# One tile a round fetched by SyncE row by row, the lows spread by ScalarE, and nodes laid out by 56 to a partition, in a graph layer on one NeuronCore

## The reference

```python
msg = relu(x[src] + edge_attr @ We + be)            # 200000 x 128
aggr = segment_sum(msg, dst, num_segments=6250)
h = (1.0 + eps) * x + aggr
h = relu(h @ W1 + b1) @ W2 + b2
h = (h - mean(h, 0)) * rsqrt(var(h, 0) + 1e-5) * gamma + beta
out = layernorm(x + (relu(h) + x))
```

## Time and profile before

| | |
|---|---|
| median of 3 runs | 1557.24 us (1556.69 to 1558.63) |
| the profiled execution | 1564.18 us, its span 1562.2 us |
| PE busy | 1416.0 us (91%), 23435 matmuls |
| ACT busy | 1255.7 us (80%) |
| POOL busy | 1160.5 us (74%), 1179 gathers |
| DVE busy | 891.9 us (57%) |
| granted TensorE clock | 0.981 of full speed over the span |
| DMA | 180.72 MB, 116 GB/s |
| chain that ended last | PE 55%, POOL 21%, issue 8%, ACT 5%, DVE 4%, DMA 4% |

### The profile page before, as it was taken

How to read it: one execution, slowest core, us unless ns; L and a number is a source line. 1 busy time by engine, 2 the same in 40 slices (tenths; PEclk the granted TensorE clock), 3 DMA queues, 4 the chain that set the end, 5 groups by cost and what they waited for, 6 DMA issues and landing times.

```text
span 1562.2 us, 60471 instructions
## 1 busy us (share of the span) xinstructions
PE 1416.0 (91%) x23435; PEld 1095.0 (70%) x23435; DVE 891.9 (57%) x3174; ACT 1255.7 (80%) x3729; POOL 1160.5 (74%) x1193
## 2 busy tenths in 40 slices
PE   1299999999999999989999999989999999999954
PEld 1277777777777777767777777767777777777734
DVE  5676665655566565555555556555556555655436
ACT  2488888888888888878877888878788888888845
POOL 7677777777777777777777777777777777777762
PEclk9999999999999999999999999999999999999967
DMA  9644445444544445444444444445444444444432
GB/s 250 170 111 109 109 113 123 113 111 117 119 113 110 108 112 126 109 106 113 111 108 106 113 106 113 112 106 117 108 110 107 111 112 107 105 112 110 104 125 84
DMA packets 148516, 180.72 MB, mean 116 GB/s; under 512 B 41725, under 2 KB 128980, under 8 KB 147972
## 3 DMA queue, kind: packets, MB, share of 16 engines
q1 hardware_dynamic: 102489, 89.62, 24.5%
q0 software_dynamic: 37728, 77.31, 20.9%
q10 hardware_dynamic: 8011, 9.90, 2.3%
HBM read 170.09 MB, written 6.63 MB: 113 GB/s over the span
## 4 chain that ended last, share of the span: by engine, by line
PE 55%; POOL 21%; issue 8%; ACT 5%; DVE 4%; DMA 4%; SPq 1%; ACTq 0%; POOLq 0%; DVEq 0%
POOL xg L590 21%; PE ps L1396 20%; PE ps L1381 14%; PE ps L1325 9%; PE ps L1311 6%; DMA xg<-xb,idxb 3%; ACT hot L747 2%; ACT msg L753 1%; PE ps L1362 1%; ACT hot L740 1%; PE ps L1342 1%; PE ps L1365 1%; PE ps L1334 1%; PE ps L1337 1%; SPq L480 1%
## 5 line engine op out<-in xcount | busy, mean ns | idle before, releaser
L590 POOL DMA_INDIRECT xg<-xb,idxb x1145 | 1107.0, 967 | 356.9 <-issue 337.0
L1396 PE MATMUL ps<-iota_all 128*128 128x128 bf16 x8064 | 518.0, 220 | 0.0
L1396 PEld LDWEIGHTS ps<-iota_all 128*128 128x128 bf16 x8064 | 452.3, 98 | 87.1 <-issue 67.7
L984 DVE TENSOR_TENSOR msg<-ps,xg 128x512 f32<-128x512 f32 x390 | 264.5, 688 | 305.6 <-DMA xg<-xb,idxb 192.8
L707 ACT ACTIVATE iota_all<-ps 128x384 bf16<-128x384 f32 x896 | 379.8, 484 | 31.7 <-PE ps L1381 28.4
L740 ACT ACTIVATE hot<-iota,rel 128x64 f32<-128x64 f32 x1560 | 391.6, 339 | 0.0
L1381 PE MATMUL ps<-x,iota_all 112*32 112x384 bf16 x7168 | 365.1, 331 | 0.0
L1069 DVE TENSOR_TENSOR accT<-accT,ps 128x64 f32 x390 | 86.2, 221 | 292.4 <-PE ps L1342 248.1
L753 ACT ACTIVATE msg<-msg 128x512 f32<-128x512 f32 x390 | 241.0, 618 | 14.7 <-DVE msg L984 14.7
L1381 PEld LDWEIGHTS ps<-x,iota_all 112*32 112x32 bf16 x7168 | 156.9, 96 | 120.6 <-issue 38.5
L1325 PE MATMUL ps<-msg,hot 128*64 128x128 f32 x3120 | 219.4, 284 | 23.1 <-ACT msg L753 23.1
(11 more groups left out here) (145 smaller groups left out, 800.3 us busy)
## 6 DMA issues: line engine op xcount, KB each, us to landing
ea<-in_eat SPq DMA_DIRECT2D x156, 320.0 KB
lowB<-lowD SPq DMA_DIRECT2D x128, 224.0 KB
xg<-xb,idxb POOLq DMA_INDIRECT x1145
accT<-in_xt ACTq DMA_DIRECT2D x1, 3125.0 KB, 14.8
x<-in_xt ACTq DMA_DIRECT2D x1, 3125.0 KB, 11.0
out<-iota_all SPq DMA_DIRECT2D x5, 512.0 KB
iota_all<-in_x ACTq DMA_DIRECT2D x3, 784.0 KB, 17.6
xb<-iota_all SPq DMA_DIRECT2D x3, 784.0 KB, 16.8
```

The source lines that it names most:

```text
L590: pool.indirect_dma_start(out=xg[0:rows, slot, j, :], out_offset=None, in_=of, in_offset=bass.IndirectOffsetOnAxis(ap=index, axis=0)).then ...
L984: add = dve.tensor_tensor(both, lin_of(half), xg[:, g % RING, :, :].rearrange("p (b t) h -> p b (t h)", b=2), ALU.add)
L1396: last = pe.matmul(found[:, e, :], sel2[set_of(k)][:, t, e * P:(e + 1) * P], rows3[:, t, a, :], start=(t == 0 and e == 0 and a == 0), stop ...
```

## The change

1. **SP fetches a tile.** In rounds 1 to 12 the last tile of group 3 (`FETCH_G`, a group not in `SORTED`) is no longer gathered by POOL. SP loads its 128 source indices into registers, 9 a step, and issues one transfer of one row (512 bytes) for each, a round ahead, into a buffer `xs` of its own. DVE's add of that group becomes three instructions. POOL issues 89 gathers in such a round where it issued 90.
2. **ACT issues the transfers of the lows.** `spread_lows` leaves SP. ACT issues `lowD<-lowS` within `keep_slots`, between its two copies, after a wait for its own first copy. It issues `lowB<-lowD` between the clip of the first group and `one_hot`, after a wait for `lowD` to have landed.
3. **Node layout.** Node n stands in partition n // 56, block n % 56. A piece is then one run of 7168 bytes a partition, moved as a transfer of 96 partitions, one of 15, and one of the last partition (34 nodes). The one-hot of a batch uses n % 28 for the block pair and the partition for the low. PE's `pick` reads block `u * 28 + m` where it read `2 * m + u`.
4. `g_msg`, used only on a path that these inputs don't take, moves into `iota_all` to make room for `xs`.

```diff
+    FETCH_G = 3
+    FETCH_ROWS = 9
         def by_pool(i, g):
-            return GROUP - HALF * special(i, g)
+            return GROUP - HALF * special(i, g) - fetched(i, g)
@@ SP
+            def fetch(i, a, b):
+                if a == 0:
+                    wait_apart(sp, s_idxs, 16 * i)
+                    if i == 1:
+                        for m in range(NQ):
+                            sp.wait_ge(s_xb[m], stores(m))
+                    if i >= 3:
+                        wait_apart(sp, s_pre, (i - 2) * ROUND + FETCH_G + 1)
+                _, node_of = nc.values_load_multi_w_load_instructions(
+                    idxs[0:1, i % 2, a:b], engines=[mybir.EngineType.SP], min_val=0, max_val=N - 1,
+                    skip_runtime_bounds_check_because="each is the src of an edge, a row of x")
+                for p in range(a, b):
+                    sp.dma_start(xs[p:p + 1, i % 2, :], xb[bass.ds(node_of[p - a], 1), :]).then_inc(s_row[i % 2], 16)
...
-                    for j, k in phase(i, q, 3):
-                        spread_lows(j, k)
+                    if i + 1 < ITERS:
+                        fetch(i + 1, q * FETCH_ROWS, min(P, (q + 1) * FETCH_ROWS))
+                    if q == STEPS - 1 and i + 2 < ITERS:
+                        load_sources(i + 2)
@@ ACT
                 act.activation(lowS[:, :], low_at, ACT.Copy).then_inc(s_low, 1)
+                if b:
+                    wait_apart(act, s_lowB, 16 * b)
+                wait_apart(act, s_low, b + 1)
+                act.dma_start(lowD.rearrange("o (b r) -> (o b) r", r=CAP), lowS[:, :]).then_inc(s_lowD, 16)
...
+            def spread_lows(j, k):
+                b = batch(j, k)
+                old = prior(j, k)
+                if old is not None:
+                    wait_apart(act, s_sel1, old + 1)
+                wait_apart(act, s_lowD, 16 * (b + 1))
+                act.dma_start(lowB[:, set_of(k), :], lowD.partition_broadcast(P)).then_inc(s_lowB, 16)
...
                     clip(n, q, 0)
+                    for j, k in phase(i, q, 3):
+                        spread_lows(j, k)
                     one_hot(q, pair)
@@ DVE, add of group 3
+                if fetched(i, g):
+                    dve.wait_ge(s_row[i % 2], 16 * P * ((i + 1) // 2))
+                    dve.tensor_tensor(to[:, 3, :], ps_lin(half, 3), xs[:, i % 2, :], ALU.add)
+                    dve.tensor_tensor(to[:, 2, :], ps_lin(half, 2), xg[:, g % RING, 2, :], ALU.add)
+                    add = dve.tensor_tensor(to[:, 0:2, :].rearrange("p t h -> p (t h)"), lin_of(half)[:, 0, :],
+                                            xg[:, g % RING, 0:2, :].rearrange("p t h -> p (t h)"), ALU.add)
@@ layout, the loads (ACT); the stores of xb (SP) have the same form
-                act.dma_start(xrow[0:SUB, a:whole, :], x[a * SUB:whole * SUB, :].rearrange("(b p) h -> p b h", p=SUB))\
-                   .then_inc(s_xrow[q], 16)
+                for c, d in ((0, MANY), (MANY, LASTP)):
+                    act.dma_start(xrow[c:d, a:b, :], x[c * NSUB:d * NSUB, :].rearrange("(p b) h -> p b h", b=NSUB)[:, a:b, :])\
+                       .then_inc(s_xrow[q], 16)
```

More of the change, by code:

```diff
@@ L81, in gine_layer_kernel @@
     NQ = len(PIECES)
+    LASTP = SUB - 1
+    MANY = LASTP // 16 * 16
+    LASTR = N - LASTP * NSUB
+    assert 0 < LASTR <= NSUB
     SORTED = (2, 5, 8, 11, 14, 17, 20, 23, 26, 29)
@@ L100, in gine_layer_kernel @@
     CLOSE = 11
+    FETCH_G = 3
+    FETCH_ROWS = 9
+    assert FETCH_ROWS * STEPS >= P and FETCH_G not in SORTED
     BANKS = (3, 7, 4)
@@ L238, in gine_layer_kernel @@
             .rearrange("p (t a h) -> p t a h", t=NTILE, a=3)
+        xs = sb("xs", [P, 2, HID])
+        idxs = sb("idxs", [1, 2, P], i32)
         g_idx = sb("g_idx", [P, 1], i32)
@@ L241, in gine_layer_kernel @@
         g_xg = sb("g_xg", [P, HID])
-        g_msg = sb("g_msg", [P, HID])
+        g_msg = iota_all[:, N + 22:N + 22 + HID]
         g_dst = sb("g_dst", [P, 4])
@@ L300, in gine_layer_kernel @@
         s_last = sem("s_last")
+        s_idxs = sem("s_idxs")
+        s_row = [sem("s_row_even"), sem("s_row_odd")]
         s_pro = sem("s_pro")
@@ L347, in stores @@
         def stores(q):
-            return 16 * (1 + (q == NQ - 1 and N % SUB > 0))
+            return 16 * (2 + (PIECES[q][0] < LASTR))
         block = ctx.enter_context(nc.Block())
@@ L401, in ending, with fetched @@
             return [(j, k) for j, k, t in visit(i, v) if t == NTILE - 1]
+        def fetched(i, g):
+            return i > 0 and g == FETCH_G
         def by_pool(i, g):
-            return GROUP - HALF * special(i, g)
+            return GROUP - HALF * special(i, g) - fetched(i, g)
         def gathered(i, g):
@@ L498, in keep_lifted @@
                 a, b = PIECES[q][0], sum(PIECES[q])
-                whole = min(b, N // SUB)
+                last = min(b, LASTR)
                 sp.wait_ge(s_lifted, q + 1)
[L501 to L517, removed]
+                for c, d in ((0, MANY), (MANY, LASTP)):
+                    sp.dma_start(xb[c * NSUB:d * NSUB, :].rearrange("(p b) h -> p b h", b=NSUB)[:, a:b, :], xrow[c:d, a:b, :])\
+                      .then_inc(s_xb[q], 16)
@@ new lines, in keep_lifted, with load_sources @@
+                if a < last:
+                    sp.dma_start(xb[LASTP * NSUB + a:LASTP * NSUB + last, :].rearrange("(p b) h -> p b h", p=1),
+                                 xrow[LASTP:SUB, a:last, :]).then_inc(s_xb[q], 16)
+            def load_sources(i):
+                e0 = (i * ROUND + FETCH_G) * GE + (GROUP - 1) * P
+                sp.dma_start(idxs[:, i % 2, :], src_row[:, e0:e0 + P]).then_inc(s_idxs, 16)
+            def fetch(i, a, b):
[11 more added lines that the diff above has]
+                    sp.dma_start(xs[p:p + 1, i % 2, :], xb[bass.ds(node_of[p - a], 1), :]).then_inc(s_row[i % 2], 16)
@@ L545, in iteration @@
                             span(i + 1, h - SPANS)
-                    for j, k in phase(i, q, 3):
-                        spread_lows(j, k)
+                    if i + 1 < ITERS:
+                        fetch(i + 1, q * FETCH_ROWS, min(P, (q + 1) * FETCH_ROWS))
+                    if q == STEPS - 1 and i + 2 < ITERS:
+                        load_sources(i + 2)
+            load_sources(1)
             run(sp, iteration)
@@ L655, in _ @@
                 a, b = PIECES[q][0], sum(PIECES[q])
-                whole = min(b, N // SUB)
-                act.dma_start(xrow[0:SUB, a:whole, :], x[a * SUB:whole * SUB, :].rearrange("(b p) h -> p b h", p=SUB))\
-                   .then_inc(s_xrow[q], 16)
-                if whole < b:
-                    act.dma_start(xrow[0:N - whole * SUB, whole, :], x[whole * SUB:N, :]).then_inc(s_xrow[q], 16)
+                last = min(b, LASTR)
+                for c, d in ((0, MANY), (MANY, LASTP)):
+                    act.dma_start(xrow[c:d, a:b, :], x[c * NSUB:d * NSUB, :].rearrange("(p b) h -> p b h", b=NSUB)[:, a:b, :])\
+                       .then_inc(s_xrow[q], 16)
+                if a < last:
+                    act.dma_start(xrow[LASTP:SUB, a:last, :],
+                                  x[LASTP * NSUB + a:LASTP * NSUB + last, :].rearrange("(p b) h -> p b h", p=1))\
+                       .then_inc(s_xrow[q], 16)
             act.dma_start(accT[:, 0:N], xt).then_inc(s_xt, 16)
@@ L808, in _ @@
                     take(j, k)
+                for j, k in phase(0, q, 3):
+                    spread_lows(j, k)
                 for j, k, t in visit(0, 2 * q + 1):
@@ L876, in _ @@
             step(dve.memset(epsc[:, 0:1], EPS))
-            step(dve.memset(xrow[:, NSUB - 1, :], 0.0))
+            step(dve.memset(xrow[LASTP // 32 * 32:SUB, LASTR:NSUB, :], 0.0))
             dve.wait_ge(s_we, 16 * 6)
@@ L954, in constants @@
                 dve.tensor_scalar(starts[:, :], iota[:, 0:NPAIR], float(CAP), None, ALU.mult)
-                dve.tensor_copy(nodeu[:, 0:1], nodes[:, 0:1])
-                dve.tensor_scalar(nodeu[:, 1:2], nodes[:, 0:1], float(SUB), None, ALU.add)
+                dve.tensor_scalar(nodeu[:, 0:1], nodes[:, 0:1], 2.0, None, ALU.mult)
+                dve.tensor_scalar(nodeu[:, 1:2], nodes[:, 0:1], 2.0, 1.0, ALU.mult, ALU.add)
             def split_sources():
                 dve.wait_ge(s_srcT, 1)
-                pair = 2.0 * SUB
+                pair = float(NPAIR)
                 source = ps[:, 3:7, :].rearrange("p a n -> p (a n)")[:, 0:LOOPED * GROUP]\
                     .rearrange("p (m c) -> p m c", c=CYCLE)[:, :, CYCLE - HALF:CYCLE]
-                step(dve.tensor_scalar(near, source, 0.5 - SUB, 1.0 / pair, ALU.add, ALU.mult))
+                step(dve.tensor_scalar(near, source, 0.5 - pair / 2, 1.0 / pair, ALU.add, ALU.mult))
                 step(dve.tensor_scalar_add(part_of, near, 12582912.0))
                 step(dve.tensor_scalar_add(part_of, part_of, -12582912.0))
```

(15 more changed lines are left out.)

5 lines of the change are left out of this document (2 added, 3 removed).

## The result

The changed kernel takes 1636.01 us (median of 4 runs, 1631.74 to 1644.17) where the kernel before takes 1557.93 (4 runs): a ratio of 1.0506, 95% interval 1.0484 to 1.0528. That is 78 us slower. I had forecast 1566 and a range up to 1598, so the size was far off. The direction agrees, but I had given "slower" only a chance of 0.50.

The account below looks back on a forecast made before the run. PE bounds pairs 0 to 75 and 143 to 183, POOL 75 to 143. With ACT's 0.25 us a pair, +4.5 by pair 143, +10 to 183, -5.8 at the end: 1557.2 + 8.7 = 1565.9, rounded to 1566 us; range 1537 to 1598.

Parts of the forecast that it names:

- What bounds the kernel: PE sets the pace to pair 75 (7.05 us a pair), POOL from 75 to 143 (7.57), PE again to 183 (7.69).
- at most 15.2: POOL, one gather less in each of 12 rounds at 1.27 us: alone gives back at most 15.2 us.
- ACT's missing slack in the step without `take`: Second clip before PE's window: only 0.06 us between them, so delays of ACT there are paid in full.
- POOL's lead: POOL starts 15 groups (7.5 pairs, 55 us) ahead, loses 0.57 us a pair to PE, lead gone at pair 75.
- The first transfer: `lowD<-lowS` on ACT before `slotS`: `slotS` starts 0.57 to 0.69 us later, costing 0.21 to 0.29 us a pair.
- The second transfer's wait: `lowB<-lowD` on ACT: wait hidden unless `lowD` lands over some 2.7 us after issue; taken as 0.02 us a pair.
- where I had 9: Clock falling from 2.4 to 1.2 GHz for short spells before pair 143: costs PE some 9 us, no longer covered.
- Before the loop: Layout starts DVE up to 9.9 us sooner, ACT stands for `lowD`; net 4.5 us sooner (0 to 9.9).
- SP's rows: Single-row fetch on SP: 0.38 us a row, 88 us a round against 106 or more; fits and costs nothing.
- At 0.58 us a row: Rival that SP can't keep up and PE waits for `ea`: about 1615 us at 0.58 a row; chance 8%.
- ACT waits for `lowD` as SP did: Rival: ACT's sequencer waits before the second transfer, 1.1 us per batch behind an `ea`, up to 47 us, about 1600; 10%.
- POOL stays the bound: Rival: ACT's delay mostly hidden, POOL's pace rules; 1537 us at 0.1 us a pair, 1550 around 0.17; chance 34%.

Follow-up runs that it names:

- ACT's order was mended: Changed kernel with `lowD` issued behind the `hot` instructions, `lowB` a step later, first three batches' lows on SP: 1543.21 us, 0.9890.
- small `ea`: Kernel before with the lows issued by ACT and four fifths of the edge attributes not loaded (old ones used): 1567.37 us, 1.0046.

## Why the prediction was right in its sign and wrong in its size

- **What bounds the kernel: right.** POOL's pace in the middle and at the end is what the fetch can win against; 14 to 15 us measured, once ACT's order was mended, against "at most 15.2". ACT's missing slack in the step without `take` is where the loss enters. One reading was off: POOL's lead ends at pair 81, where the first long cycle begins, and the prediction's own 55 us of lead at 0.57 a pair would have lasted to pair 96, not 75. The sum does not hang on it.
- **The first transfer, 0.21 to 0.29 us a pair: the mechanism right, the size just under the range.** `slotS` 0.66 us after `lowS` (forecast 0.66 to 0.78), quiet cycle 21.73 us (forecast 21.8 to 22.1), so 0.19 a pair.
- **The second transfer's wait, 0.02 us a pair: this is the step that failed.** That would be 3 us up to pair 143. In that stretch ACT stood 45.0 us for `lowD`, 33 times, 0.31 a pair; in the whole run 51.7 us, 39 times. The pace there is 7.70 us against 7.24 in quiet cycles, 0.45 a pair or 65 us. Besides the 45 it holds seven short spells at 1.2 GHz, 27 us together (granted clock 0.99 in that stretch), which by my estimate cost up to half their length, 14 us where I had 9. Some 6 us stay without a cause. The first transfer adds 28. Of these 93 us, 36 had been the price of POOL's pace and the clock in the kernel before (1043.9 - 143 x 7.05), and 57 are the loss; this is bookkeeping of the two paces, not a separate proof. The proof is in the runs: with `lowB` a step later 43 us of that stretch come back, and with small `ea` 53 against the lows on ACT alone (7.28 a pair for 7.65). Both keep the full clock all through it, so they hold the clock's part as well.

  I had the limit right (landing 2.7 us after the issue), and had the case in my rows: 3.8 us between the two issues 2.9 us after an `ea`. I explained it by SP's queue and so set the term near 0, drawing on the Trainium skill ("DMA: Bandwidth & Descriptors", Queues, rings and completion order), by which an engine takes turns between queue rows. On a queue of its own `lowD` landed as late; with small `ea` it did not. No run shows in which order an engine serves its rows, but turns between rows did not give the landing of a quiet queue here. By the row alone my price was 47 us, a third of the batches at 1.1 us each, which I gave 10%; it was 39 of 128 at 1.3. Where a row and a rule name different ends, the sum should have stood nearer the row.
- **Before the loop: wrong.** Forecast 4.5 us gained, 2.6 lost. The layout gives nothing; POOL still waits 5.9 us for `xb`. ACT's first stand for `lowD` took 10.4 us, not 2 to 3. With those batches on SP that stand is gone and pair 0 came 3.3 us earlier. Why this first `lowD` lands so late is open. On ACT's queue it came after `xt` (3.1 MB), which had landed at 39.5 us, and after a last 64 KB of weights, which landed at 48.0, just before ACT could go on at 48.6. But on SP's queue, behind the stores of `xb`, the same transfer took as long (timeline of that run), so what the move to SP gained is that ACT no longer stands for it:

```profile
46.28 0.31 SPq L549 DMA_DIRECT2D lowD<-lowS  x1
57.21 0.35 SPq L554 DMA_DIRECT2D lowB<-lowD  x1
```

  In the changed kernel the DMA engines were busy throughout between 36 and 52 us (a share of 0.97 to 1.11 by the profile's count).
- **SP's rows: right.** Nine rows took 3.56 us, 0.40 each (0.38 taken), and SP still waited 314.6 us for PE, 75 times. (At 0.58 us a row the prediction's own steps give about 1622, not 1615.) The queue's records of the changed kernel, ns min/median/max:

```profile
L541 SPq DMA_DIRECT2D xs<-xb x1536: 217/228/397, 58.0 to 1473.7; - x192
...
L537 SPq TENSOR_LOAD <-idxs x180: 657/2068/2319, 56.8 to 1472.4; - x180
```

- **Rivals.** "ACT waits for `lowD` as SP did" was the true one. Its 1600 falls short of 1636 by the longer waits, the start (7 us later than forecast), the clock, pairs 143 to 183, and the baseline: the profiled executions differ by 68 us, the medians by 78. "POOL stays the bound" is what happens once ACT's order is mended: 1543, close to its 1537, though that was not the kernel it was said of.

## What to carry to other kernels

When a computing engine issues a transfer, look first at the wait in front of the issue. Here that wait cost the most, while an issue was free only where other instructions already filled the engine's queue: put the issue behind such instructions, and the wait a step after the transfer that it waits for. Before a small transfer is moved, read how long it takes to land next to the large ones, in its worst case, and compare that with the slack of the engine that is to wait; here 4.2 us met 2.7. The waits of the engine that had the transfer before are a good place for it: SP's 278.3 us in 120 waits were 2.3 each. And where two engines are within 0.1 us of each other in a cycle, price every delay in full.

## What the runs showed of the hardware

- A small transfer (28 rows of 64 bytes) issued 2 to 4 us after 640 KB on the other engine's queue landed in 4.2 us in the median, as on the same queue (4.1), against 1.7 to 1.8 away from it. Its packets started late: the last 2.9 to 3.0 us after the issue, against 1.1.
- A transfer of one 512-byte row, its address in a register, held SP's queue 0.228 us, less than the 0.33 of the larger small ones; a row with its register arithmetic took 0.40.
- Loading nine registers (one TENSOR_LOAD row) took 2.07 us in the median, more than half of what the nine rows themselves took, and hung on the address. In the 48 loads whose first index stands a multiple of 16 bytes from the start of its buffer (steps 0, 4, 8 and 12 of a round) the median was 0.94 us, in the other 120 it was 2.13. DVE's loads of ten registers took 1.06 to 1.09 or 2.29 to 2.31 us in turn, the long ones at 8 bytes off such a multiple.
- 1536 such transfers beside the rest left the time unchanged (1636.0 with them, 1637.7 without).
